# Attention denominators in a fused conv / linear attention / expert kernel: guard on ScalarE, power of minus one on GpSimd, in place of guard and reciprocal on VectorE

## Chip, cores, metric

One Trainium2 chip, one of its cores. The metric is the device time of one execution, in microseconds. An execution takes some 4.5 ms, and the executions shown of the kernel before lie within 0.07% of each other.

## What is computed

Sixteen images of 64 channels and 56x56 pixels pass three residual blocks: a convolution block, linear attention over the 3136 pixels (tokens) with 16 heads, and a block of 32 experts. The change touches the attention block only, and there the denominators:

```python
q = jax.nn.elu(q) + 1.0; k = jax.nn.elu(k) + 1.0
q_cos, q_sin = q * cos, q * sin; k_cos, k_sin = k * cos, k * sin
kv_cos = einsum('bshx,bshz->bhxz', k_cos, v); kv_sin = einsum('bshx,bshz->bhxz', k_sin, v)
qkv = einsum('bshx,bhxz->bshz', q_cos, kv_cos) + einsum('bshx,bhxz->bshz', q_sin, kv_sin)
denom = 1.0 / (einsum('bshd,bhd->bsh', q_cos, k_cos.sum(axis=1))
             + einsum('bshd,bhd->bsh', q_sin, k_sin.sum(axis=1)) + 1e-05)
o = qkv * denom[..., None]
out = o.reshape(b, s, h * d) @ dense_w.T + dense_b
```

The 1e-05 is "the guard", and 1/(...) the reciprocal.

## The kernel before

The images are worked on in eight **pairs**, two images on the 128 partitions. A hardware loop runs seven pairs ("loop"), the eighth is written out behind it ("last"). One pair has a k phase (key features and their products), a **q phase** and a tail (second layer norm, routing, then the convolution block of the next pair). The change lies in the q phase.

The q phase takes the pixels in chunks of 448 (8 rows of an image), 7 for each image, so 14 chunks, called s = 0 to 13 (`STEPS` is 14). The engines each run their own instruction queue in order, and a software pipeline over **steps** s = 0 to 16 is written out by hand in each of them. In step s, chunk s gets its query features, chunk s-1 its denominators, chunk s-2 is scaled and multiplied by the output matrices, and chunk s-3 is folded into the residual Y. Steps 14 to 16 drain the pipeline. Within a step a counter cc = 0 to 4 sets the places.

What happens to one chunk, by engine and line:

- TensorE projects the queries, in four parts of 256 features (L1375, banks A and B in turn, cc = 0 to 3). ScalarE takes exp (L688, into EQ), and VectorE makes the feature from both (L1010 `q_features`, into Q). L1010 empties the bank.
- TensorE forms partial denominators (L1392, bank E), VectorE multiplies them by cos and sin (L1027 `den_parts`, into DS), TensorE sums them (L1403 `q_sums`, into bank C, 96 partitions x 224 values: two halves of the chunk, 16 heads, in three copies).
- VectorE adds the guard (L1033 `den_guard`, bank C into RR[:, 0], which empties the bank) and takes the reciprocal (L1040 `den_reciprocal`, RR[:, 0] into RR[:, 1]).
- GpSimd splits the reciprocal in three bf16 parts, RS3 (L544, L546, L550, L551, L553: "the split").
- TensorE spreads the parts over the channels (L1417 `q_broadcast`, four times for a chunk, through bank C), and VectorE scales the features by it (L1019 `q_scale`, four times). "Broadcast cc" and "scale cc" below are the cc-th of these.
- TensorE multiplies the scaled features by the output matrices (L1428 `q_output`, bank D, once after each scale; "output cc"), VectorE multiplies by cos and sin (L1046 `out_parts`), TensorE folds (L1438 `q_fold`, bank C), and VectorE adds to Y (L1054 `out_residual`, "the residual").

Bank C is one PSUM area that serves these in a fixed order within a step: broadcast 0, sums, fold, broadcasts 1, 2, 3. Each use waits until the one before has been emptied. RR and RS3 are small SBUF tiles; RR has one buffer.

Between these, VectorE works through the depthwise convolution of the next pair (L855, in the seven loop pairs, 1, 1, 1, 2, 2 pieces at cc = 0 to 4; the last pair has none). In steps 12 and 14 these are replaced by parts of the second layer norm (L896 to L904), whose input comes through bank C at the end of steps 11 and 13 (TensorE L1264, ScalarE L589). In step 13 ScalarE takes the square root for it (L596 `deviations`, right after the exp of cc = 0), and VectorE applies it at cc = 2 (L916, L917). The square root and the exp need different function tables on ScalarE, so a table load stands ahead of each.

VectorE waits in L1010 at cc = 0, s >= 3, until output 3 of chunk s-3 is done, since both use the same buffer of Q.

## Time and profile before

| | |
|---|---|
| time, median of 3 | 4513.36 us (4513.25 to 4516.37) |
| profiled execution, its own time | 4506.9 us |
| its span | 4505.0 us |
| mean granted TensorE clock | 0.971 |
| PE / DVE / ACT / POOL busy | 3877.1 / 3434.0 / 1340.9 / 497.9 us |
| one steady step of the q phase (s = 3 to 11) | 18.2 us |

PE is TensorE's matmul pipe, PEld its weight load, DVE VectorE, ACT ScalarE, POOL GpSimd. "Busy" adds up over all stages, and stages have different limits. So the table says which engine works most over the whole, not which one sets the pace of the q phase. That is read in the rows below: from how long a step takes, and from the chain of work in it.

### The profile page before, as it was taken

Reading aid. Unit: us, or ns where it says so; the run is one execution under the profiler, and the core shown is the slowest. Engines: PE = TensorE matmul, PEld = TensorE weight load, DVE = VectorE, ACT = ScalarE, POOL = GpSimd, SP = SyncE. Lnnn points to the kernel's source line nnn. Section 1 sums busy time; section 2 is a strip of 40 time slices with the busy share of each in tenths; the row PEclk is TensorE's granted clock in tenths of the full one; section 3 lists DMA queues with packets and bytes.
Section 4 is the critical chain, followed back from the end, with each engine's and each line's share of the span. In section 5 each row is a group of like instructions: output and inputs, shape, how many; then the busy total and the mean of one; then the engine's idle time right before and its main releaser. Section 6 shows DMA issues by size and latency. Waiting matters only on the chain.

```text
span 4505.0 us, 48667 instructions
## 1 busy us (share of the span) xinstructions
PE 3877.1 (86%) x15836; PEld 1865.8 (41%) x15836; DVE 3434.0 (76%) x4533; ACT 1340.9 (30%) x1432; POOL 497.9 (11%) x977
## 2 busy tenths in 40 slices
PE   4998889987998889988899879988899888998876
PEld 2443344433543335433444335433354334443353
DVE  6688886888778886888868887788868888556633
ACT  0152233422253223522334222532235223342220
POOL 0011100111011110111001110111101110011100
PEclk8999999999999999999999999999999999999967
DMA  1000000000000001000000000000010000100035
GB/s 43 15 1 1 1 15 23 1 1 1 22 16 1 1 1 37 1 1 1 15 23 1 1 1 22 16 1 1 1 37 1 1 1 15 27 1 1 1 101 185
DMA packets 18779, 70.61 MB, mean 16 GB/s; under 512 B 8797, under 2 KB 13565, under 8 KB 13629
## 3 DMA queue, kind: packets, MB, share of 16 engines
q1 hardware_dynamic: 18509, 67.16, 4.8%
q8 instruction: 151, 2.47, 0.2%
q14 instruction: 119, 0.97, 0.1%
HBM read 37.32 MB, written 29.84 MB: 15 GB/s over the span
## 4 chain that ended last, share of the span: by engine, by line
PE 68%; DVE 19%; issue 8%; ACT 4%; DMA 1%; SPq 1%; DVEq 0%; ACTq 0%
PE ps_D L1428 16%; DVE region L1019 7%; PE ps_C L1346 6%; PE ps_D L1227 4%; PE ps_D L1346 4%; PE ps_E L1346 4%; PE ps_A L1331 4%; DVE arena L855 3%; PE ps_B L1331 3%; PE ps_A L1375 3%; PE ps_C L1253 3%; PE ps_C L1417 2%; PE ps_C L1403 2%; PE ps_C L1438 2%; PE ps_E L1392 2%
## 5 line engine op out<-in xcount | busy, mean ns | idle before, releaser
L1428 PE MATMUL ps_D<-region,small 128*128 128x448 f32 x1792 | 793.7, 567 | 171.5 <-DVE region L1019 171.5
L855 DVE SCALAR_TENSOR_TENSOR arena<-arena,W8C 128x448 f32<-128x448 f32 x1344 | 876.3, 692 | 0.9
L1428 PEld LDWEIGHTS ps_D<-region,small 128*128 128x128 f32 x1792 | 320.8, 193 | 535.1 <-DVE region L1019 349.2
L1019 DVE TENSOR_TENSOR region<-region,ps_C 128x896 f32<-128x896 f32 x400 | 433.1, 1083 | 80.8 <-PE ps_C L1417 69.3
L688 ACT ACTIVATE EQ<-ps_A,NEG 128x896 f32<-128x896 f32 x224 | 225.7, 1008 | 832.4 <-PE ps_A L1375 832.4
L532 POOL TENSOR_TENSOR UA<-region,CS 128x128 f32<-128x128 f32 (+1 forms) x400 | 192.0, 482 | 1924.6 <-DVE region L924 908.5
L688 ACT ACTIVATE EQ<-ps_B,NEG 128x896 f32<-128x896 f32 x224 | 225.6, 1007 | 598.1 <-PE ps_B L1375 598.0
L1346 PE MATMUL ps_C<-region,UA 128*128 128x512 f32 (+1 forms) x800 | 378.1, 595 | 0.0
L987 DVE SCALAR_TENSOR_TENSOR region<-region,ps_A 128x1024 f32<-128x1024 f32 (+1 forms) x200 | 243.8, 1219 | 122.8 <-ACT region L666 121.1
L987 DVE SCALAR_TENSOR_TENSOR region<-region,ps_B 128x1024 f32<-128x1024 f32 (+1 forms) x200 | 243.8, 1219 | 109.8 <-ACT region L666 107.4
L1010 DVE SCALAR_TENSOR_TENSOR region<-EQ,ps_A 128x896 f32<-128x896 f32 x224 | 242.6, 1083 | 82.5 <-ACT EQ L688 43.3
L666 ACT ACTIVATE region<-ps_A,NEG 128x1024 f32<-128x1024 f32 (+1 forms) x200 | 222.9, 1114 | 263.5 <-PE ps_A L1331 263.4
L666 ACT ACTIVATE region<-ps_B,NEG 128x1024 f32<-128x1024 f32 (+1 forms) x200 | 223.0, 1115 | 248.8 <-PE ps_B L1331 248.6
L544 POOL CAST RS<-RR 96x224 bf16<-96x224 f32 x112 | 57.1, 510 | 1829.0 <-DVE RR L1040 1813.3
L1403 PE MATMUL ps_C<-DS,SEL 128*96 128x224 f32 x448 | 118.2, 389 | 161.1 <-DVE region L1019 152.9
L1417 PE MATMUL ps_C<-RS,SELB 96*128 96x224 bf16 x1600 | 224.1, 263 | 29.4 <-ACT un L589 16.3
L1010 DVE SCALAR_TENSOR_TENSOR region<-EQ,ps_B 128x896 f32<-128x896 f32 x224 | 242.3, 1082 | 8.2 <-ACT EQ L688 7.1
L1392 PE MATMUL ps_E<-region,small 128*32 128x448 f32 x1792 | 214.9, 551 | 37.1 <-DVE region L1010 37.1
L1227 PE MATMUL ps_D<-region 112*128 112x512 f32 x496 | 214.8, 593 | 11.7 <-ACT region L631 11.7
L1417 PEld LDWEIGHTS ps_C<-RS,SELB 96*128 96x128 bf16 x1600 | 148.5, 99 | 180.2 <-issue 110.5
L1346 PE MATMUL ps_D<-region,UA 128*128 128x512 f32 (+1 forms) x400 | 205.9, 596 | 0.0
L1346 PE MATMUL ps_E<-region,UA 128*128 128x512 f32 (+1 forms) x400 | 204.2, 592 | 0.0
(310 smaller groups left out, 5792.4 us busy)
## 6 DMA issues: line engine op xcount, KB each, us to landing
arena<-x SPq DMA_DIRECT2D x8, 1568.0 KB, 6.8
t_keep<-Y SPq DMA_DIRECT2D x7, 1568.0 KB, 5.2
w_keep<-region SPq DMA_DIRECT2D x7, 784.0 KB, 5.9
CST<-t_keep SPq DMA_DIRECT2D x2, 1568.0 KB, 10.2
small<-t_keep SPq DMA_DIRECT2D x2, 1568.0 KB, 13.7
plane<-w_keep SPq DMA_DIRECT2D x4, 784.0 KB, 16.0
UHL<-t_keep SPq DMA_DIRECT2D x2, 1568.0 KB, 13.2
out<-CST SPq DMA_DIRECT2D x2, 1568.0 KB, 12.2
```

Source lines behind the costliest of these rows:

```text
L666: act.activation(E[0:r, k % 2], here.area(("kp", k))[0:r, :], ACT.Exp, bias=NEG1[0:r, 0:1]).then_inc(e_ready.sem, 1)
L688: act.activation(EQ[:, cc % 2], here.area(key)[:, :] .rearrange("p (c n) -> p c n", c=2)[:, :, 0:PIX], ACT.Exp, bias=NEG1[:, 0:1]).then_in ...
L855: dve.scalar_tensor_tensor(out=chunk, in0=window, scalar=w[:, k:k + 1], in1=chunk, op0=ALU.mult, op1=ALU.add).then_inc(taps_done.sem, 1)
L987: dve.scalar_tensor_tensor(out=KT[0:r, k % 3], in0=E[0:r, k % 2], scalar=1.0, in1=here.area(key)[0:r, :], op0=ALU.min, op1=ALU.max)\
L1010: dve.scalar_tensor_tensor(out=Q[s % 3][:, 2 * cc:2 * cc + 2, :], in0=EQ[:, cc % 2], scalar=1.0, in1=here.area(key)[:, :].rearrange("p (c ...
L1019: dve.tensor_tensor(out=q, in0=q, op=ALU.mult, in1=here.area(key)[:, :].rearrange("p (c n) -> p c n", c=2)[:, :, 0:PIX])\
L1227: ins = pe.matmul(here.area("t3")[:, :], UCOL[0:HALFP, j, :], UCOL[0:HALFP, j:j + 7:2, :], start=j == 0, stop=j == SPLIT - 1)
L1331: ins = pe.matmul(here.area(key)[0:r, cut], UTS[i][:, t * P:t * P + r], w[:, cut], start=m == 0, stop=m == 1)
L1346: ins = pe.matmul(dst, UA[0:r, k % 3].rearrange("p s c -> p (s c)"), KT[0:r, k % 3, n * 512:(n + 1) * 512], start=t == 0, stop=t == TILES - 1)
L1392: ins = pe.matmul(here.area(key)[j * STRIP:(j + 1) * STRIP, 0:PIX], KK[i][:, c, :], Q[s % 3][:, c, :], start=g == 0, stop=g == 1)
L1417: ins = pe.matmul(here.area(key)[:, at:at + SUB], SELB[:, j, 2 * c:2 * c + 2, :].rearrange("p h c -> p (h c)"), RS3[:, s % 2], start=True, ...
L1428: ins = pe.matmul(here.area(key)[:, 0:PIX], MW[i][:, c, :], Q[s % 3][:, c, :], start=c == 0, stop=c == NCHUNK - 1)
```

## The change

ScalarE adds the guard. It does so behind its exp of cc = 0, as an `Identity` activation with the 1e-05 as bias, from bank C into RR[:, 0], and that now empties the bank. It first waits for the split of the chunk before, since RR[:, 0] has one buffer. GpSimd then takes RR[:, 0] to the power of -1 (two-input instruction, the second input a broadcast column of -1) into RR[:, 1], ahead of its split. VectorE's two instructions are gone. Nothing else moves.

```diff
                 for s in range(STEPS):
+                    pool.wait_ge(*here.emptied(("dsum", s)))
+                    pool.tensor_tensor(out=RR[:, 1], in0=RR[:, 0], in1=NEG1[0:96, 0:1].broadcast_to([96, SUB]), op=ALU.pow).then_inc(recip_ready.sem, 1)
                     pool.wait_ge(*recip_ready.at(pair, s + 1))
...
+            def den_guard(here, s):
+                key = ("dsum", s)
+                if s >= 1:
+                    act.wait_ge(*split_ready.at(here.pair, s))
+                    passed(act)
+                act.wait_ge(*here.filled(key))
+                act.activation(RR[:, 0], here.area(key)[0:96, 0:SUB], ACT.Identity, bias=EPS[0:96, 0:1])\
+                    .then_inc(*here.empty(key))
...
                                            ACT.Exp, bias=NEG1[:, 0:1]).then_inc(eq_ready.sem, 1)
+                        if cc == 0 and 1 <= s <= STEPS:
+                            den_guard(here, s - 1)
                         if cc == 0 and s - 2 in LN2_STEPS[:2]:
                             deviations(ln2_sums, ln2_std, pair, LN2_STEPS.index(s - 2))
...
-            def den_guard(here, s):
-                dve.wait_ge(*here.filled(("dsum", s)))
-                dve.tensor_scalar(RR[:, 0], here.area(("dsum", s))[0:96, 0:SUB], DEN_EPS, None, ALU.add)\
-                    .then_inc(*here.empty(("dsum", s)))
-
-            def den_reciprocal(here, s):
-                dve.wait_ge(*here.emptied(("dsum", s)))
-                if s >= 1:
-                    dve.wait_ge(*split_ready.at(here.pair, s))
-                dve.reciprocal(RR[:, 1], RR[:, 0]).then_inc(recip_ready.sem, 1)
...
-                        if cc == 1 and 1 <= s <= STEPS:
-                            den_guard(here, s - 1)
                         if cc == 1 and s >= 3 and not drain:
                             out_residual(here, s - 3)
-                        if cc == (1 if drain else 2) and 1 <= s <= STEPS:
-                            den_reciprocal(here, s - 1)
```

The lines of the changed kernel are shifted: exp is L700 there, the guard L669, the square root L598, the power L540.

ScalarE's queue in step 13 of a loop pair, before (exp of cc = 0, square root with its table loads, exp of cc = 1 and 2):

```order
L688 ACTIVATE EQ<-ps_A,NEG1 128x896 [waits ps_A_filled]
L595 REGISTER_ALU
L596 ACT_TABLE_LOAD
L596 ACTIVATE ST<-ST,EPS 128x14 [waits ln2_sums]
L687 REGISTER_ALU
L688 ACT_TABLE_LOAD
L688 ACTIVATE EQ<-ps_B,NEG1 128x896 [waits ps_B_filled]
```

And in the changed kernel, same place:

```order
L700 ACTIVATE EQ<-ps_A,NEG1 128x896 [waits ps_A_filled]
L666 REGISTER_ALU
L668 REGISTER_ALU [waits split_ready]
L669 ACTIVATE RR<-ps_C,EPS 96x224 [waits ps_C_filled]
L597 REGISTER_ALU
L598 ACT_TABLE_LOAD
L598 ACTIVATE ST<-ST,EPS 128x14 [waits ln2_sums]
L699 REGISTER_ALU
L700 ACT_TABLE_LOAD
L700 ACTIVATE EQ<-ps_B,NEG1 128x896 [waits ps_B_filled]
```

The guard has come in between the exp of cc = 0 and all that follows it, the table loads, the square root and the exp of cc = 1, and it waits for the sums (ps_C_filled). In the other steps it stands at the same place, ahead of the exp of cc = 1, without table loads. No table load has been added anywhere in ScalarE's queue.

VectorE's queue in a steady step before, from the features of cc = 1 to those of cc = 2 and the reciprocal:

```order
L1010 SCALAR_TENSOR_TENSOR region<-EQ,ps_B 128x896 [waits eq_ready]
L1032 REGISTER_ALU
L1033 TENSOR_SCALAR RR<-ps_C 96x224 [waits ps_C_filled]
L1053 REGISTER_ALU
L1054 SCALAR_TENSOR_TENSOR Y<-ps_C,DBC,Y 64x448 [waits ps_C_filled]
L844 REGISTER_ALU
L855 SCALAR_TENSOR_TENSOR arena<-arena,W8C 128x448 [waits taps_done]
L1018 REGISTER_ALU
L1019 TENSOR_TENSOR region<-region,ps_C 128x896 [waits ps_C_filled]
L1007 REGISTER_ALU
L1010 SCALAR_TENSOR_TENSOR region<-EQ,ps_A 128x896 [waits eq_ready]
L1039 REGISTER_ALU [waits ps_C_emptied]
L1040 RECIPROCAL RR<-RR 96x224 [waits split_ready]
```

In the changed kernel the rows of L1032, L1033, L1039 and L1040 are missing there and the rest stands as it was; the residual (L1054) follows the features of cc = 1 directly. GpSimd's queue has the power ahead of each split:

```order
L539 REGISTER_ALU
L540 TENSOR_TENSOR RR<-RR,NEG1 96x224 [waits ps_C_emptied]
L541 REGISTER_ALU
L546 CAST RS3<-RR 96x224 [waits recip_ready]
L547 REGISTER_ALU
L548 TENSOR_TENSOR RR<-RR,RS3 96x224 [waits gstep]
```

Before, the first two of these rows were not there, and the cast waited for VectorE.

## Rows read from the trace of the kernel before

**Rows 1.** Profile page, busy time and share of the span by engine.
```profile
PE 3877.1 (86%) x15836; PEld 1865.8 (41%) x15836; DVE 3434.0 (76%) x4533; ACT 1340.9 (30%) x1432; POOL 497.9 (11%) x977
```

**Rows 2.** One step by windows: a loop pair's, the last pair's; busy us, PEclk.
```profile
core 0: us, PE busy (x) PEld busy (x) DVE busy (x) ACT busy (x) POOL busy (x), PEclk, DMA share, GB/s
432.39:450.61 18.22, 15.18 (x71) 6.82 (x70) 16.12 (x21) 4.03 (x4) 2.43 (x5) 1.00 0.00 1
4142.50:4160.92 18.42, 15.22 (x71) 6.83 (x72) 12.02 (x13) 4.03 (x5) 2.31 (x5) 1.00 0.00 1
```

**Rows 3.** Chain of work through that steady step: start us, us, what.
```profile
436.07 1.00 PE ps_C L1403 x4
...
440.83 1.10 DVE region L1019
...
444.93 1.10 DVE region L1019
...
449.87 1.72 PE ps_D L1428 x4
```

**Rows 4.** Timeline of the same step: start us, us, engine, line, operation, [idle before].
```profile
436.52 1.08 DVE L1010 SCALAR_TENSOR_TENSOR region<-EQ,ps_B 128x896 f32<-128x896 f32 x1
437.52 0.38 DVE L1033 TENSOR_SCALAR RR<-ps_C 96x224 f32<-96x224 f32 x1
...
439.50 0.68 DVE L1054 SCALAR_TENSOR_TENSOR Y<-ps_C,DBC,Y 64x448 f32<-64x448 f32 x1 [1.60 <-PE ps_C L1438]
...
444.62 0.49 POOL L544 CAST RS<-RR 96x224 bf16<-96x224 f32 x1 [15.41 <-DVE RR L1040]
...
446.82 0.60 POOL L553 TENSOR_TENSOR RS<-RR,RS 32x224 bf16<-32x224 f32 x1
```

**Rows 5.** Instructions by line: ns min/median/max, first and last start, form.
```profile
L1040 DVE RECIPROCAL RR<-RR x112: 1539/1542/1550, 372.5 to 4287.4; 96x224 f32<-96x224 f32 x112
L546 POOL TENSOR_TENSOR RR<-RR,RS x112: 605/607/1433, 374.9 to 4289.6; 96x224 f32<-96x224 f32 x112
...
L688 ACT ACTIVATE EQ<-ps_B,NEG x224: 1000/1007/1009, 358.3 to 4272.5; 128x896 f32<-128x896 f32 x112
...
L709 ACT ACTIVATE region<-ps_B,GBC x23: 629/630/632, 652.2 to 4328.9; 64x448 f32<-64x448 f32 x23
```

**Rows 6.** Timeline of step 12 of the first pair, and its clock by windows.
```profile
566.48 1.00 PE L1403 MATMUL ps_C<-DS,SEL 128*96 128x224 f32 x4 [2.33 <-DVE region L1019]
...
570.20 0.69 DVE L1054 SCALAR_TENSOR_TENSOR Y<-ps_C,DBC,Y 64x448 f32<-64x448 f32 x1 [1.06 <-PE ps_C L1438]
...
572.14 1.09 DVE L1019 TENSOR_TENSOR region<-region,ps_C 128x896 f32<-128x896 f32 x1
...
577.12 1.09 DVE L1019 TENSOR_TENSOR region<-region,ps_C 128x896 f32<-128x896 f32 x1 [0.49 <-DVE SQ L902]
...
578.26 3.23 PE L1428 MATMUL ps_D<-region,small 128*128 128x448 f32 x4 [2.07 <-DVE region L1019]
...
580.00:582.00 2.00, 2.00 (x7) 0.89 (x7) 0.20 (x1) 0.00 (x0) 0.00 (x0) 0.54 0.00 0
```

**Rows 7.** Timeline of step 13 of the first pair.
```profile
583.93 1.28 ACT L596 ACT_TABLE_LOAD   x1
...
586.85 1.01 ACT L688 ACTIVATE EQ<-ps_B,NEG 128x896 f32<-128x896 f32 x1
...
591.60 0.69 DVE L1054 SCALAR_TENSOR_TENSOR Y<-ps_C,DBC,Y 64x448 f32<-64x448 f32 x1 [1.60 <-PE ps_C L1438]
...
593.04 1.09 DVE L1019 TENSOR_TENSOR region<-region,ps_C 128x896 f32<-128x896 f32 x1
...
598.28 1.08 DVE L1019 TENSOR_TENSOR region<-region,ps_C 128x896 f32<-128x896 f32 x1
```

**Rows 8.** Timeline of steps 1 and 2 of the first pair.
```profile
368.25 0.99 PE L1403 MATMUL ps_C<-DS,SEL 128*96 128x224 f32 x4 [1.17 <-DVE DS L1027]
...
378.31 0.93 PE L1417 MATMUL ps_C<-RS,SELB 96*128 96x224 bf16 x4 [1.74 <-POOL RS L553]
...
380.11 1.07 DVE L1019 TENSOR_TENSOR region<-region,ps_C 128x896 f32<-128x896 f32 x1
```

## Prediction

> **What bounds the kernel now.** I read the busy times first. TensorE leads over the whole kernel, VectorE is second with 76% [rows 1], and inside the q phase VectorE is the fuller engine: 16.12 of 18.22 us of a steady step against TensorE's 15.18 [rows 2]. That makes relieving VectorE look worth while. The second row of the same view speaks against it. The last pair has no depthwise pieces, VectorE is busy for only 12.02 us there, and the step still takes 18.42 us. So four microseconds less VectorE work bought nothing. The steady step isn't limited by VectorE's amount of work.
>
> The chain of work shows what limits it [rows 3]. It goes sums, output 0, fold, broadcast 1, scale 1 (starts 440.83), output 1, projection, broadcast 2, scale 2 (444.93), output 2, broadcast 3, projection, partial denominators, output 3 (449.87 to 451.59), and through the features of cc = 0, the cos/sin product and scale 0 to the next sums. TensorE's instructions in order with VectorE's scales between them. In this step neither L1033 nor L1040 is in the chain. I call the start of the sums T; here T = 436.07 [rows 3], and the step repeats every 18.2 us.
>
> **Removing the reciprocal.** 112 reciprocals of 1.54 us [rows 5] and 112 guards of 0.38 us [rows 4] are 215 us of VectorE work. In a steady step the reciprocal stands between scale 1 and scale 2. Their distance is 4.10 us [rows 3], and TensorE fills it (output 1, projection, broadcast 2), so without the reciprocal VectorE would only wait there. Gain: 0.
>
> **Moving the guard.** What ended the guard's wait is no longer in VectorE's queue but in ScalarE's, ahead of the exp of cc = 1, which used to be ready early. What is queued behind it: that exp, then the features of cc = 1, then the residual on VectorE, and broadcast 1 on TensorE, which needs bank C back from the residual. Step by step from T: the sums take 1.00 us [rows 3]; 0.04 us to wake ScalarE (my allowance for a hand-over; the table says the same order for all of them); the guard; the exp, 1.01 us [rows 5]; 0.03 us; and the features, after which VectorE starts its next instruction 1.00 us later (436.52 to 437.52, [rows 4]). The guard's size isn't in the trace. An Identity with bias from PSUM takes 0.63 us for 448 columns and an exp 1.01 us for 896 [rows 5], 0.84 ns a column, which makes 0.44 us for 224. The two rows bound it, at 0.44 us by that line and 0.63 us by the larger Identity. I take 0.44. The sum is 1.00 + 0.04 + 0.44 + 1.01 + 0.03 + 1.00 = T + 3.52. The residual starts now at 439.50 = T + 3.43 [rows 4], held there by the fold, not by VectorE (1.60 us idle). So the new path is 0.09 us later, and if neighbouring ScalarE instructions overlap a little, equal. I take 0.05 us for each of the 72 steady steps (s = 3 to 11 of eight pairs): **+3.6 us**, bounds -7 (-0.1 a step; VectorE runs into fewer collisions) and +22 (+0.3 a step, the larger guard and slow hand-overs).
>
> **Step 12** is the one kind of step that VectorE does bound. The norm's parts stand in its queue, and scale 1 to scale 2 takes 572.14 to 577.12 = 4.98 us [rows 6] instead of 4.10 [rows 3]. Without the reciprocal TensorE's 4.10 becomes the distance: -0.88. The residual comes 3.72 us after the sums (566.48, 570.20) and could come at 3.52: -0.2. Together -1.1 in seven pairs, less in the last, about **-8 us**. Behind it hangs more. After the idle 2.07 us TensorE's granted clock is 0.54 in this stretch, near the lower level, 1.2 GHz, and output 2 takes 3.23 us [rows 6] where the same line has 1.72 us in a steady step [rows 3]. With the shorter gap this dip may go, some 1.6 us in each of 7 pairs: another **-11**. I think that likely (3 in 4).
>
> **Step 13** is where the new order hurts. ScalarE's square root stands behind the exp of cc = 0, with table loads on both sides. From the first load (583.93) to the exp of cc = 1 (586.85) pass 2.92 us [rows 7], and today they lie beside VectorE's and TensorE's work of the step's start. In the changed kernel they stand behind the guard, and that waits for the sums. So: 1.00 + 0.04 + 0.44 + 2.92 + 1.01 + 0.03 + 1.00 = T + 6.44 for the residual, which is at 591.60 today, T + 3.43 as ever: +3.0 us. The reciprocal's absence gives back part: scale 1 to scale 2 takes 5.24 us here (593.04 to 598.28, [rows 7]), and TensorE allows 4.10: -1.1. Net +1.9 in eight pairs: **+15 us**. TensorE idles for 3 us ahead of broadcast 1, longer than the 2.07 us after which it ran at 0.54 in step 12 [rows 6]. A dip of the same price, 1.6 us in eight pairs, is likely: **+13**. Bounds of the step: +12 and +30.
>
> **The power on GpSimd** has no row at all. The nearest is the two-input subtraction of the same shape on the same engine, 0.605 us [rows 5], and that is the lower end. [...] If that is ten such passes it takes 6 us, and at twenty 12 us. VectorE pays four times its simple instruction for the reciprocal (1.54 against 0.38), which would give 2.5 us here. I take 6 us and keep 0.6 to 12. When is it felt? In a steady step the power can start at about T + 1.7. The split after it takes 444.62 to 447.42 = 2.80 us [rows 4], with some 0.2 us of hand-overs. The next step's broadcast 0 comes behind output 3, at 451.5 = T + 15.4. So up to 10.7 us are free, and I cost it at nothing there; beyond that each microsecond lengthens every step by as much. In steps 1 and 2 there is less room: sums from 368.25, so the power starts at about 369.9, the split after it takes 3 to 4 us, and scale 0 at 380.11 needs broadcast 0 (0.93 us) to have begun by 379.1 [rows 8]. That leaves 5.1 to 6.2 us. With 6 us it costs 0.5 us a pair, a little more in the last: **+5**; at 3 us 0, at 10 us +36.
>
> The Trainium skill speaks against the move (GPSIMD Engine Reference, sections 3.1 and 4.1): elementwise work belongs on VectorE, GpSimd being about two times slower with two inputs, and a body with data-dependent branches costs about 12 cycles an element. Worked out from that page's 1.2 GHz, 224 elements would take 2.2 us, an estimate. By it the +5 above would be 0 and the time 4 or 5 us lower; no row here shows what the power's body is.
>
> **The sum.** 3.6 - 8 - 11 + 15 + 13 + 5 = +18 us. Leaving both clock terms out gives +16, so they hardly matter together, only if one comes without the other. Against the profiled execution's own 4506.9 us (span 4505.0) that is 4525; against the median, 6.5 us higher, 4531. I give 4530.
>
> **Rivals.**
> (a) *The relief counts: faster.* VectorE's queue would bind in the steady steps too, as it nearly does in loop pairs (16.12 of 18.22 busy). If all 1.92 us counted in the loop's 63 steady steps, it would be 4513 - 121 = 4392. It decides from the point where the residual after the guard is not held by the fold. The last pair's step of 18.42 us at 12.02 us busy [rows 2] speaks against it. A mild form is the step 12 term alone with its clock and a step 13 that costs little: -19 + 12 - 7 = -14, 4500. Together 0.12.
> (b) *No change.* The power is short (under 5 us), step 12 gives its 19 us back, and step 13 costs 15 without a dip: 3.6 - 19 + 15 = 0, so 4513. For it speaks that step 13 was idle for 2 us in places today without a dip. 0.26.
> (c) *GpSimd becomes the bound: much slower.* The power takes over 10.7 us. At 14 us each of some 100 steps is 3.3 us longer, +330, 4840. No row excludes it; only a body of more than seventeen elementary passes would do it. 0.14.
> (d) *The change doesn't do what it says*, by table loads around the new Identity. ScalarE's order shows none added, so under 0.01.
> (e) My forecast, with the power between 3 and 10.7 us and step 13 with or without a dip: 4522 to 4575. 0.48.
>
> **How the numbers follow.** Likeliest 4530. Range: down to the mild form of (a) and up to a power of nearly 10.7 us with the guard's upper bound: 4500 to 4590. That leaves out (c) and the strong form of (a). A difference under 0.2% (9 us) can't be told from none by a measurement of this kernel. Faster by more: 0.12. Within: 0.26. Slower: 0.62.
>
> **What would show it.** Right: the steady step stays at 18.2 to 18.3 us, with VectorE's busy time 1.9 us lower and an idle stretch of about 2 us ahead of the features of cc = 1, ended by the exp; step 12 shorter, by 1 us or by 2.7 with the full clock; step 13 longer by 2 to 4 us, with the table loads after the sums. Wrong: a steady step below 18 us would mean that VectorE had bound it; a steady step of 20 us or more with broadcast 0 waiting for L555 would mean a power over 10.7 us; and a residual later than T + 3.6 in the steady step would put the guard's path higher than I have it.

## The result: 62% slower, by the length of one GpSimd instruction

The changed kernel takes 7323.7 us (median of 4, 7321.6 to 7328.0) against 4513.3 us, a ratio of 1.623 with an interval of 1.620 to 1.626. That is 2810 us more. The forecast was 4530 us; the run went the way of rival (c), and much further than it was priced.

The page of the changed kernel: busy time and share of the span by engine; the granted clock in 40 slices; the chain by engine and line; and the costliest group (busy us, mean ns of one, idle before it).

```profile
PE 4100.0 (56%) x15836; PEld 1973.2 (27%) x15836; DVE 3237.5 (44%) x4309; ACT 1376.3 (19%) x1544; POOL 4494.1 (61%) x1089
...
PEclk9967789677986679866797668967789777987776
...
POOL 60%; issue 32%; PE 5%; DVE 1%; DMA 1%; POOLq 0%; ACT 0%; SPq 0%; DVEq 0%; ACTq 0%
...
L540 POOL TENSOR_TENSOR RR<-RR,NEG 96x224 f32<-96x224 f32 x112 | 4034.0, 36018 | 665.2 <-ACT RR L669 665.2
```

One power takes 36.0 us. GpSimd is the busiest engine with 61%, where it had 11% [rows 1], and the power alone is 4034 us in 112 instructions. VectorE has 224 instructions fewer, and its busy time fell by 197 us (3434.0 to 3237.5), somewhat less than the 215 us that the prediction had counted for them. Nobody profited.

One steady step of the changed kernel, timeline (start us, us, engine, line, operation, [idle before <- what ended it]):

```profile
585.46 0.44 ACT L669 ACTIVATE RR<-ps_C,EPS 96x224 f32<-96x224 f32 x1 [30.29 <-PE ps_C L1402]
585.98 36.02 POOL L540 TENSOR_TENSOR RR<-RR,NEG 96x224 f32<-96x224 f32 x1 [4.53 <-ACT RR L669]
...
589.30 0.56 PE L1416 MATMUL ps_C<-RS,SELB 96*128 96x224 bf16 x4
...
622.53 0.37 POOL L546 CAST RS<-RR 96x224 bf16<-96x224 f32 x1 [0.53 <-POOL RR L540]
...
624.60 0.60 POOL L555 TENSOR_TENSOR RS<-RR,RS 32x224 bf16<-32x224 f32 x1
625.25 0.93 PE L1416 MATMUL ps_C<-RS,SELB 96*128 96x224 bf16 x4 [24.62 <-POOL RS L555]
...
626.22 1.09 DVE L1033 TENSOR_TENSOR region<-region,ps_C 128x896 f32<-128x896 f32 x1 [23.93 <-PE ps_C L1416]
...
627.47 1.70 PE L1402 MATMUL ps_C<-DS,SEL 128*96 128x224 f32 x4
...
629.21 0.44 ACT L669 ACTIVATE RR<-ps_C,EPS 96x224 f32<-96x224 f32 x1 [30.12 <-PE ps_C L1402]
...
629.73 36.02 POOL L540 TENSOR_TENSOR RR<-RR,NEG 96x224 f32<-96x224 f32 x1 [4.53 <-ACT RR L669]
```

This is a closed loop: the power (36.02), the split (622.53 to 625.20), broadcast 0, scale 0, the sums, the guard, and the next power, 43.75 us after the last here, 43.46 in most steps and on average over the steady ones. All of TensorE's and VectorE's other work of a step has long been done when broadcast 0 waits 24.6 us for the split. After this pause TensorE runs slowly. Broadcast 0 takes 0.93 us where broadcast 1 of the step before took 0.56 (at 589.30), and the sums take 1.70 us instead of 1.00 [rows 3]. The windows show the granted clock: 0.50, the level of 1.2 GHz, from 625.2 to 629.2 us, and 1.00 from 588.4 to 600.0. The mean granted clock of the run is 0.787 against 0.971. The ScalarE wait of 30 us ahead of the guard costs nothing by itself; it is the same pause, seen from another queue.

The prediction had worked out that a step has room for a power of 10.7 us and that each microsecond beyond counts in full. 18.2 + (36.0 - 10.7) = 43.5 us, and 43.46 was measured. Times 111 that is 2808 us. So the mechanism was right, the threshold nearly so (experiment 3 puts it a little higher), and one number, the length of the power, was wrong by a factor of six.

That the sum meets the measurement to 0.04 us is in part luck. Its 10.7 came from three pieces of the loop outside the power: 1.7 us from the start of the sums to the power, 3.0 from the power to broadcast 0, and 2.8 from broadcast 0 to the next sums. In the step shown they are 2.26 (the sums before started at 583.72), 3.25 and 2.22 us, together 7.73 instead of 7.5, and 7.44 on average. The slow clock made the first longer, and the third is shorter since scale 0 no longer waits behind VectorE's other work.

### The profile page after: what moved, and what is told of

It is laid out like the page before. It is cut to its first block, busy times and chain, and to the rows that moved or that the text cites. A ratio compares the mean times of both kernels' runs of the same rounds, so it can differ in the third digit from the quotient of the medians.

```text
span 7326.2 us, 48856 instructions
## 1 busy us (share of the span) xinstructions
PE 4100.0 (56%) x15836; PEld 1973.2 (27%) x15836; DVE 3237.5 (44%) x4309; ACT 1376.3 (19%) x1544; POOL 4494.1 (61%) x1089
## 4 chain that ended last, share of the span: by engine, by line
POOL 60%; issue 32%; PE 5%; DVE 1%; DMA 1%; POOLq 0%; ACT 0%; SPq 0%; DVEq 0%; ACTq 0%
POOL RR L540 55%; POOL UA L532 2%; POOL RR L548 1%; POOL RS L555 1%; PE ps_C L1345 1%; POOL RS L553 1%; POOL RS L546 1%; PE ps_A L1530 0%; PE ps_D L1226 0%; PE ps_A L1330 0%; PE ps_D L1345 0%; PE ps_E L1345 0%; PE ps_B L1330 0%; PE ps_C L1402 0%; DMA plane<-w_keep 0%
## 5 line engine op out<-in xcount | busy, mean ns | idle before, releaser
L540 POOL TENSOR_TENSOR RR<-RR,NEG 96x224 f32<-96x224 f32 x112 | 4034.0, 36018 | 665.2 <-ACT RR L669 665.2
L1416 PE MATMUL ps_C<-RS,SELB 96*128 96x224 bf16 x1600 | 264.7, 297 | 2800.9 <-POOL RS L555 2777.9
L1033 DVE TENSOR_TENSOR region<-region,ps_C 128x896 f32<-128x896 f32 x400 | 435.0, 1088 | 2871.9 <-PE ps_C L1416 2863.1
L1427 PE MATMUL ps_D<-region,small 128*128 128x448 f32 x1792 | 842.5, 596 | 149.8 <-DVE region L1033 149.8
L869 DVE SCALAR_TENSOR_TENSOR arena<-arena,W8C 128x448 f32<-128x448 f32 x1344 | 858.6, 678 | 0.9
L669 ACT ACTIVATE RR<-ps_C,EPS 96x224 f32<-96x224 f32 x112 | 49.6, 443 | 3121.8 <-PE ps_C L1402 3121.8
L1427 PEld LDWEIGHTS ps_D<-region,small 128*128 128x128 f32 x1792 | 355.0, 212 | 547.8 <-DVE region L1033 330.2
L700 ACT ACTIVATE EQ<-ps_A,NEG 128x896 f32<-128x896 f32 x224 | 225.4, 1006 | 541.1 <-PE ps_A L1374 541.0
L700 ACT ACTIVATE EQ<-ps_B,NEG 128x896 f32<-128x896 f32 x224 | 224.1, 1000 | 366.8 <-PE ps_B L1374 366.7
## 6 DMA issues: line engine op xcount, KB each, us to landing
CST<-t_keep SPq DMA_DIRECT2D x2, 1568.0 KB, 10.7
```

Of the source, the lines that this page charges most:

```text
L540: pool.tensor_tensor(out=RR[:, 1], in0=RR[:, 0], in1=NEG1[0:96, 0:1].broadcast_to([96, SUB]), op=ALU.pow).then_inc(recip_ready.sem, 1)
L700: act.activation(EQ[:, cc % 2], here.area(key)[:, :] .rearrange("p (c n) -> p c n", c=2)[:, :, 0:PIX], ACT.Exp, bias=NEG1[:, 0:1]).then_in ...
L869: dve.scalar_tensor_tensor(out=chunk, in0=window, scalar=w[:, k:k + 1], in1=chunk, op0=ALU.mult, op1=ALU.add).then_inc(taps_done.sem, 1)
L1033: dve.tensor_tensor(out=q, in0=q, op=ALU.mult, in1=here.area(key)[:, :].rearrange("p (c n) -> p c n", c=2)[:, :, 0:PIX])\
L1416: ins = pe.matmul(here.area(key)[:, at:at + SUB], SELB[:, j, 2 * c:2 * c + 2, :].rearrange("p h c -> p (h c)"), RS3[:, s % 2], start=True, ...
L1427: ins = pe.matmul(here.area(key)[:, 0:PIX], MW[i][:, c, :], Q[s % 3][:, c, :], start=c == 0, stop=c == NCHUNK - 1)
```

## Experiments

**1. The power replaced by a multiplication.** Is the power the whole loss, and does the rest of the sum hold?

```diff
-pool.tensor_tensor(out=RR[:, 1], in0=RR[:, 0], in1=NEG1[0:96, 0:1].broadcast_to([96, SUB]), op=ALU.pow)
+pool.tensor_tensor(out=RR[:, 1], in0=RR[:, 0], in1=NEG1[0:96, 0:1].broadcast_to([96, SUB]), op=ALU.mult)
```

> The changed kernel, but GpSimd multiplies by -1 where it took the power of -1, so the reciprocal is left out and the denominators are wrong. Everything else of the change stays. Theory (the power's length is the whole loss, the rest of my sum holds): the multiplication takes 0.6 us, a steady step 18.2 to 18.3 us, step 12 is 1 to 2.7 us shorter and step 13 is 2 to 4 us longer than before; time 4513 + 3.6 - 8 - 11 + 15 + 13 = 4526, between 4505 and 4545. Rival (VectorE had bound the steady step after all, and only the power hid that): a steady step near 16.3 us and a time near 4392. Rival (the guard's new place costs by itself much more than I had it): over 4600.

Measured: 4557.9 us (5 runs), ratio 1.0096 (1.008 to 1.011), 41 us more than before on the same chip, and 13 us above the range expected. So some 98.5% of the loss is the power's length. It is the operation, too: the multiplication has the same operands, the broadcast column among them, and takes 0.56 us. The steady step is 18.21 us, as before and as forecast. Its timeline (same columns) and its windows row (span, then PE, PEld, DVE, ACT and POOL busy, PEclk):

```profile
437.74 1.00 PE L1402 MATMUL ps_C<-DS,SEL 128*96 128x224 f32 x4 [1.56 <-DVE region L1033]
438.78 0.44 ACT L669 ACTIVATE RR<-ps_C,EPS 96x224 f32<-96x224 f32 x1 [5.29 <-PE ps_C L1402]
439.12 0.99 ACT L700 ACTIVATE EQ<-ps_B,NEG 128x896 f32<-128x896 f32 x1
439.30 0.56 POOL L540 TENSOR_TENSOR RR<-RR,NEG 96x224 f32<-96x224 f32 x1 [14.13 <-ACT RR L669]
...
440.15 1.09 DVE L1024 SCALAR_TENSOR_TENSOR region<-EQ,ps_B 128x896 f32<-128x896 f32 x1 [1.87 <-ACT EQ L700]
...
441.18 0.68 DVE L1057 SCALAR_TENSOR_TENSOR Y<-ps_C,DBC,Y 64x448 f32<-64x448 f32 x1
```
```profile
434.50:452.71 18.21, 15.18 (x72) 6.82 (x71) 14.28 (x19) 4.36 (x5) 3.46 (x6) 1.00 0.00 1
```

The guard takes 0.44 us. The residual starts at 441.18, 3.44 us after the sums, where the kernel before had 3.43 [rows 3, 4]. VectorE's busy time in the step fell from 16.12 to 14.28 us; there is now a wait of 1.87 us ahead of the features of cc = 1, and the step is the same to a hundredth. The rival that VectorE had bound the steady step is out.

Step by step, from the distances between VectorE's cos/sin products of the denominators (L1027 before, L1041 here) in the second pair:

| stretch of one loop pair | before | multiplication |
|---|---|---|
| steps 1 and 2 | 11.08 + 17.25 | 10.57 + 16.29 |
| a steady step | 18.21 | 18.21 |
| step 12 | 24.22 | 21.62 |
| step 13 | 19.46 | 23.88 |
| step 14 to the next pair's step 1 | 289.8 | 295.8 |

Step 12 gains 2.6 us, the forecast with its clock term (2.7): output 2 behind a pause of 1.18 us takes 1.77 us there, at a granted clock of 1.00. Step 13 loses 4.4 us, of which 1.9 plus 1.6 were forecast. Its rows, from the first pair:

```profile
588.76 1.00 PE L1402 MATMUL ps_C<-DS,SEL 128*96 128x224 f32 x4 [1.56 <-DVE region L1033]
...
589.80 0.44 ACT L669 ACTIVATE RR<-ps_C,EPS 96x224 f32<-96x224 f32 x1 [5.29 <-PE ps_C L1402]
590.26 1.28 ACT L598 ACT_TABLE_LOAD   x1
...
591.88 1.28 ACT L700 ACT_TABLE_LOAD   x1
593.17 1.01 ACT L700 ACTIVATE EQ<-ps_B,NEG 128x896 f32<-128x896 f32 x1
...
595.33 0.69 DVE L1057 SCALAR_TENSOR_TENSOR Y<-ps_C,DBC,Y 64x448 f32<-64x448 f32 x1
...
596.08 0.93 PE L1416 MATMUL ps_C<-RS,SELB 96*128 96x224 bf16 x4 [3.06 <-DVE Y L1057]
```

Both table loads stand behind the guard, and the residual comes at T + 6.57 (worked out: 6.44). Broadcast 1 behind the 3.06 us pause takes 0.93 us, so the dip that was called likely was there.

The last line of the table was not in the prediction at all: 6 us in each of seven pairs, 43 of the 55 us that lie between the two profiled executions (spans 4505.0 and 4559.7 us). I come back to it in experiment 7.

**2. Half of the columns.** Does the power's length go by the columns, or is there a large fixed part? The power is on columns 0 to 111, the multiplication on the rest.

```diff
+pool.tensor_tensor(out=RR[:, 1, 0:112], in0=RR[:, 0, 0:112], in1=NEG1[0:96, 0:1].broadcast_to([96, 112]), op=ALU.pow)
+pool.tensor_tensor(out=RR[:, 1, 112:SUB], in0=RR[:, 0, 112:SUB], in1=NEG1[0:96, 0:1].broadcast_to([96, SUB - 112]), op=ALU.mult)
```

> The changed kernel with the power on the first 112 of 224 columns and a multiplication by -1 on the other 112; half of the reciprocals are left out. The kernel with a multiplication on all columns took 4558. Theory (160.8 ns for each column, no large fixed part; 10.7 us free in a step): the power takes 18.0 us, the multiplication some 0.35 us, and a steady step is 18.2 + (18.4 - 10.7) = 25.9 us; the time is 4558 plus 111 times 7.7 = 5410. Rival (a large fixed cost for each power, a program fetched for it, for instance): the power stays far above 18 us and the time lies nearer to 7324.

Measured: 5358.6 us, ratio 1.189 (1.187 to 1.191). The steady steps are 24.9 to 26.7 us long, 26.0 on average, where 25.9 was expected.

**3. 64 columns.** The same with 64 in place of 112 puts the power where the prediction had the threshold.

> The same with the power on 64 columns and a multiplication on 160; the other reciprocals are left out. Theory (10.7 us are free in a steady step, about 5.6 us in steps 1 and 2): power 10.3 us and multiplication 0.45 us, together 10.75, so a steady step of 18.2 to 18.4 us, step 1 to 2 longer by 5 us in each pair, time 4558 + 41 + up to 10 = 4599 to 4610. Rival (the power's length counts in full from the first microsecond, since GpSimd's queue is in series with the rest): 4558 plus 111 times 10.1 = 5680.

Measured: 4593.7 us, ratio 1.0194 (1.0181 to 1.0207). Against the multiplication's 1.0096 that is about 1% or 44 us more for 10.4 us more on GpSimd in each of 112 steps; in series it would have been over 1100. From step 5 on the steady steps are 18.21 us again. The cost sits in step 2, some 22.3 us in place of 16.3 in six of the eight pairs, and there in step 3 (18.9 to 20.4). The 44 us are a net figure: in the profiled executions steps 1 to 13 lost some 58 us against experiment 1, while the tail took 289.9 us in five of its six full intervals and gave 34 us back. Power and multiplication take 10.52 + 0.45 = 10.97 us. With 10.7 us free the steady step should have been 18.5 us. Broadcast 0 does wait 0.45 us for the split there, but scale 0 is still held by VectorE's other work:

```profile
475.13 0.56 PE L1417 MATMUL ps_C<-RS,SELB 96*128 96x224 bf16 x4 [0.45 <-POOL RS L556]
...
476.25 1.08 DVE L1034 TENSOR_TENSOR region<-region,ps_C 128x896 f32<-128x896 f32 x1
```

So about eleven microseconds are free in a steady step, a little more than the prediction had, and about five in the first ones, as it had it.

**4. A third of the partitions.** The power is on partitions 0 to 31, all columns; two multiplications do the other 64.

```diff
+pool.tensor_tensor(out=RR[0:32, 1], in0=RR[0:32, 0], in1=NEG1[0:32, 0:1].broadcast_to([32, SUB]), op=ALU.pow)
+pool.tensor_tensor(out=RR[32:64, 1], in0=RR[32:64, 0], in1=NEG1[32:64, 0:1].broadcast_to([32, SUB]), op=ALU.mult)
+pool.tensor_tensor(out=RR[64:96, 1], in0=RR[64:96, 0], in1=NEG1[64:96, 0:1].broadcast_to([32, SUB]), op=ALU.mult)
```

> The power on 32 of the 96 partitions, all 224 columns, and a multiplication by -1 on the other 64 in two instructions of 32 partitions (the reciprocals there are left out). Theory (the length goes by columns only): the power takes 36.0 us as in the changed kernel, the time is 7324 plus 112 times 1.2 us of multiplications = 7460. Rival (the length goes by the number of values): 12 us, a step of 18.2 + (13.2 - 10.7) = 20.7 us, time near 4840.

Measured: 7507 us (one run), 47 us above the 7460 expected. The power keeps its length. The power in the changed kernel and in experiments 2 to 4 (line, ns min/median/max, first and last start, form):

```profile
L540 POOL TENSOR_TENSOR RR<-RR,NEG x112: 36017/36017/36027, 369.1 to 7076.2; 96x224 f32<-96x224 f32 x112
```
```profile
L540 POOL TENSOR_TENSOR RR<-RR,NEG x112: 18197/18197/18207, 370.8 to 5125.1; 96x112 f32<-96x112 f32 x112
```
```profile
L540 POOL TENSOR_TENSOR RR<-RR,NEG x112: 10524/10525/10535, 369.5 to 4365.7; 96x64 f32<-96x64 f32 x112
```
```profile
L540 POOL TENSOR_TENSOR RR<-RR,NEG x112: 36005/36006/36015, 369.4 to 7252.5; 32x224 f32<-32x224 f32 x112
```

(36.017 - 18.197) / 112 = 159 ns a column, (18.197 - 10.525) / 48 = 160 ns, and 0.3 us are left as a fixed part. A third of the partitions takes the same time.

**5. The guard on ScalarE alone.** The reciprocal stays on VectorE, so only the guard's new place is measured.

```diff
 # ScalarE, behind the exp of cc = 0
+den_guard(here, s - 1)
 # VectorE
-den_guard(here, s - 1)
```

> Only the guard moves to ScalarE, at the place that it has in the changed kernel; the reciprocal stays on VectorE at the place of before, and GpSimd does the split alone. Theory (my working of the guard's path): steady step 18.2 to 18.3 us (+3.6 us in all), step 13 longer by 3.0 us and perhaps by another 1.6 us by the clock, since the reciprocal's absence gives nothing back; time 4513 + 4 + 24 = 4541, up to 4554. Rival (ScalarE has so much room, 30% busy, that moving the guard is free): 4513 plus or minus 5.

Measured: 4563.2 us, ratio 1.0107 (1.0089 to 1.0124), 47 us more than before, where 28 to 41 were expected. Steady steps 18.21 us: the guard's path is free there. The two profiled executions lie 55 us apart. Step 13 takes 22.8 to 24.2 us in the loop pairs against 19.46, so 3.3 to 4.7 us more, and 22.1 against 19.9 in the last, 29 us in all. Steps 1 and 2 are together 10 us longer over the eight pairs, for which the prediction had nothing. The tail adds 17 us: it was 295.8 us in three of the seven intervals, 289.3 in three, and 286.8 in the last one (before: 287.1), which has the written-out pair behind it. The guard's path through a steady step was sized well; the guard is a loss mostly by its place in step 13.

**6. The guard one place later,** behind the exp of cc = 1, with the multiplication in place of the power.

```diff
-if cc == 0 and 1 <= s <= STEPS:
+if cc == 1 and 1 <= s <= STEPS:
     den_guard(here, s - 1)
```

> The changed kernel with the multiplication by -1 in place of the power (reciprocal left out), and the guard one place later in ScalarE's queue, behind the exp of cc = 1. Theory (step 13 is longer because table loads, square root and exp stand behind the guard's wait): step 13 falls from 23.9 us to 18.4 or below, since those no longer wait for the sums and VectorE's reciprocal is gone; steps 12 and the steady ones keep their 21.6 and 18.2 us. Rival (step 13 is long for another reason, the shorter step 12 or the clock): it stays above 22 us.

Measured: 4477.8 us, ratio 0.991 (0.989 to 0.993), faster than before by 0.9%, without the reciprocal. Step 13 is 18.33 us in every loop pair. Step 12, which I had expected to stay at 21.6 us, takes 23.2 in most pairs. Of the 79 us between the profiled executions of this kernel and of experiment 1, 45 are step 13 and 39 are the tail, which ran at 289.4 us in all intervals but the first. ScalarE's rows in step 13:

```profile
582.52 1.28 ACT L598 ACT_TABLE_LOAD   x1
...
584.14 1.28 ACT L700 ACT_TABLE_LOAD   x1
...
585.43 1.01 ACT L700 ACTIVATE EQ<-ps_B,NEG 128x896 f32<-128x896 f32 x1
...
587.79 0.44 ACT L669 ACTIVATE RR<-ps_C,EPS 96x224 f32<-96x224 f32 x1 [1.35 <-PE ps_C L1402]
```

Loads and exp are done before the sums are, and the guard waits for them with nothing urgent behind it. The cause of the longer step 13 is thereby shown: the place in the queue, not the table loads as such.

**7. The tail.** Its work is the same in all these kernels. Two windows of 24 us that begin some 4 us ahead of the token pooling, in the kernel before and with the multiplication (busy us by engine, PEclk):

```profile
1213.60:1237.60 24.00, 23.32 (x118) 14.88 (x117) 4.51 (x13) 1.61 (x3) 0.00 (x0) 1.00 0.00 1
```
```profile
1225.49:1249.49 24.00, 23.33 (x101) 16.99 (x100) 3.88 (x12) 1.61 (x3) 0.00 (x0) 0.72 0.00 1
```

And the 64-column matmuls of the token pooling that stand there, before and with the multiplication (ns min/median/max):

```profile
L1300 PE MATMUL ps_E<-region,un x350: 272/275/320, 692.2 to 3851.9; 128*128 128x64 f32 x168, 64*128 64x64 f32 x7
```
```profile
L1299 PE MATMUL ps_E<-region,un x350: 275/421/473, 697.0 to 3902.1; 128*128 128x64 f32 x168, 64*128 64x64 f32 x7
```

TensorE was busy 97% of both windows, at clocks of 1.00 and 0.72, and got 118 matmuls done in one and 101 in the other. In all seven tails of the multiplication the clock fell within a microsecond of the first matmul of the pooling. Ahead of that matmul TensorE pauses twice, 0.45 and 0.22 us, with the clock at 1.00, and it has the same pauses in the kernel before, where the clock stays. The fall costs 6 us. I thought that fuller work in between would hold the clock up, and put six matmuls of 128x448 f16 into the pooling.

```diff
     ins = pe.matmul(here.area("pool")[:, 0:C], UT[2][0:r, t, :], WT[0:r, t, :], start=t == 0, stop=t == TILES - 1)
+    if t in (5, 11, 17) and here.span == "loop":
+        for a in range(2):
+            pe.matmul(ps["D"][:, 0:PIX], WQH[:, 0:P], WKH[:, 0:PIX], start=True, stop=True)
```

> The kernel with the multiplication (reciprocal left out), and in the tail of each loop pair six more matmuls of 128x448 f16 (two each at three places among the 25 64-column matmuls of the token pooling), whose result nobody reads. The kernel without them spends 295.8 us from the last cos/sin product of denominators of a pair to the first of the next, the kernel before 289.7 us, and the granted clock in the pooling and the first convolutions is 0.70 to 0.73 against 1.00. Theory (the clock falls there when the stretch of small matmuls meets it at a bad phase, and fuller work keeps it up): the stretch takes 289.7 + 6 x 0.19 = 290.8 us at clock 1.00, and the kernel's time falls by 7 times 5 = 35 us against the one without. Rival (the tail is longer for a reason of the change itself): it stays near 296 or becomes 297 us.

Measured: 4577.3 us, ratio 1.0125 (1.0102 to 1.0147), and the tail took 298.5 us in its six full intervals. The fillers added their own time and held nothing. But they came too late to test the theory. The first matmul of the pooling, the first two fillers, and the clock by windows (PEclk is the third number from the end):

```profile
1237.27 2.07 PE L1299 MATMUL ps_E<-region,un 128*128 128x64 f32 x12 [0.22 <-ACT region L625]
1239.12 0.95 PE L1303 MATMUL ps_D<-WKH,WQH 128*128 128x448 f16 x2
```
```profile
1235.10:1237.10 2.00, 1.49 (x19) 1.09 (x17) 1.32 (x6) 1.57 (x3) 0.00 (x0) 1.00 0.04 8
1237.10:1239.10 2.00, 1.83 (x12) 1.84 (x13) 0.85 (x3) 0.04 (x1) 0.00 (x0) 0.75 0.00 0
1239.10:1241.10 2.00, 2.00 (x11) 1.74 (x10) 0.00 (x0) 0.00 (x0) 0.00 (x0) 0.50 0.00 0
```

The clock had fallen before the first filler ran. So the experiment shows only that fillers behind the fall don't bring the clock back sooner; whether fuller work ahead of it would have held the clock stays untested. What stays is the observation: in the profiled execution of the kernel before all seven tails ran at full clock (289.7), with the multiplication none did (295.8), and with the guard alone four did and three didn't, within one execution and with the same instructions. What decides it isn't settled.

**8. Scale 0 first.** The chain of the kernel before [rows 3] has TensorE's longest idle stretch, 1.56 us, ahead of the sums, behind three VectorE instructions of which only the last, scale 0, is needed. If the step is this chain, reordering them should pay where taking away work doesn't. Guard and reciprocal are on VectorE, as before.

```diff
+q_scale(here, s - 2, 0)
-q_features(here, s, 0)
 out_parts(here, s - 3)
-q_scale(here, s - 2, 0)
+q_features(here, s, 0)
```

> The kernel before (guard and reciprocal on VectorE) with one thing reordered: at the start of a step (cc = 0, steps 2 to 13) VectorE does scale 0 first, then the cos/sin product of the outputs, then the features of cc = 0; before, the features came first and the scale last. Theory (the steady step is TensorE's chain with VectorE's scales in it, and its longest idle stretch, 1.56 us ahead of the sums, is VectorE's three instructions): scale 0 starts as soon as broadcast 0 is done, at 433.78 instead of 434.94, so a step is shorter by about 1.1 us and the time by 1.1 times 80 = 90 us, near 4425. Rival (VectorE's amount of work bounds the loop pairs' steps, 16.1 of 18.2 us): the step gets only some 0.3 us shorter there and 1.1 us in the last pair alone, time near 4480.

Measured: 4519.5 us, ratio 1.0029 (1.0018 to 1.004), slightly slower. The step went to 18.06 us in the loop pairs and 17.6 in the last one. The steps of the profiled execution gained 32 us in all, and its tails of 296 to 299 us took back 58. My expectation of 17.1 us was wrong. A row of the loop pair's step tells why:

```profile
436.85 0.97 PE L1440 MATMUL ps_C<-OS,FOLD 128*64 128x448 f32 x2 [0.92 <-DVE RR L1033]
```

The sums come a microsecond earlier, and now the fold waits 0.92 us for VectorE's guard to empty bank C, since the guard still stands behind the same queue. With the fillers of experiment 7 added it was 4528 us, ratio 1.000 (0.997 to 1.003). Eleven of its twelve executions lay between 4474 and 4536 us. In the profiled one a single tail ran at full clock, so this one says no more of the fillers than experiment 7 does. What was expected of it:

> The reordered kernel (guard and reciprocal on VectorE, scale 0 first), with the same six matmuls in the tail. Without them it was 0.3% slower than the kernel before, with steps shorter by 0.15 to 0.8 us and a tail of 296 to 299 us. Theory (it was slower only by the clock in the tail): tail 291 us, time 0.6 to 1.0% below the kernel before. Rival (the fillers don't hold the clock): slower than before by 0.3 to 0.5%.

**9. Scale 0 first, on the changed kernel with the multiplication.**

```diff
-if feature and cc < 4:
-    q_features(here, s, cc)
+if scaled and cc == 0 and not drain:
+    q_scale(here, s - 2, 0)
 if cc == 0 and s >= 3 and not drain:
     out_parts(here, s - 3)
-if scaled and cc == 0:
+if feature and cc < 4:
+    q_features(here, s, cc)
+if scaled and cc == 0 and drain:
     q_scale(here, s - 2, 0)
...
-pool.tensor_tensor(out=RR[:, 1], in0=RR[:, 0], in1=NEG1[0:96, 0:1].broadcast_to([96, SUB]), op=ALU.pow)
+pool.tensor_tensor(out=RR[:, 1], in0=RR[:, 0], in1=NEG1[0:96, 0:1].broadcast_to([96, SUB]), op=ALU.mult)
```

> The changed kernel with the multiplication by -1 in place of the power (reciprocal left out) and, in addition, scale 0 first in VectorE's step, as in the reordered kernel. That kernel's steady step was 18.06 us in loop pairs and 17.6 us in the last pair, where VectorE has no depthwise pieces. Theory (once TensorE's chain is shorter, VectorE's amount of work is the next bound, and only then its relief is worth something): with 1.9 us less on VectorE the loop pairs' step falls to 17.6 to 17.7 us, as in the last pair. Rival (something else holds the loop pairs' step): it stays at 18.06 us. The guard's path adds at most 0.1 us in either case.

Measured: 4437.9 us, ratio 0.982 (0.980 to 0.985). The step fell to 17.07 us, further than the theory said. That left two readings: less work on VectorE, or the guard no longer in its queue.

**10. A complete kernel from the parts.** The guard on ScalarE behind the exp of cc = 1, the reciprocal on VectorE, scale 0 first. It also separates the two readings, for here VectorE keeps 1.54 us of the 1.92.

Against the changed kernel, beside the reordering shown in experiment 9:

```diff
 # GpSimd
-pool.tensor_tensor(out=RR[:, 1], in0=RR[:, 0], in1=NEG1[0:96, 0:1].broadcast_to([96, SUB]), op=ALU.pow)
 # ScalarE
-if cc == 0 and 1 <= s <= STEPS:
+if cc == 1 and 1 <= s <= STEPS:
     den_guard(here, s - 1)
 # VectorE
+def den_reciprocal(here, s):
+    dve.wait_ge(*here.emptied(("dsum", s)))
+    if s >= 1:
+        dve.wait_ge(*split_ready.at(here.pair, s))
+    dve.reciprocal(RR[:, 1], RR[:, 0]).then_inc(recip_ready.sem, 1)
...
+if cc == (1 if drain else 2) and 1 <= s <= STEPS:
+    den_reciprocal(here, s - 1)
```

> A complete kernel made of what the runs so far showed: the guard on ScalarE, but behind the exp of cc = 1; the reciprocal on VectorE as before; scale 0 first in VectorE's step. Theory (the steady step is TensorE's chain; in the reordered kernel the fold waited 0.92 us for VectorE's guard, and with the guard on ScalarE that wait goes; the reciprocal lies beside TensorE's 4.1 us and costs nothing): steady step 17.1 to 17.3 us, step 13 not above 20 us, tail 290 to 299 us by the clock; time 1.0 to 1.8% below the kernel before. Rival (VectorE's amount of work, 15.7 us with the reciprocal, holds the step of the loop pairs): steady step 17.7 to 18.0 us, time 0 to 0.6% below.

Measured: 4393.9 us (4392.6 to 4396.9), ratio 0.973 (0.971 to 0.974), 2.7% faster than before, with the whole computation in it. That is more than the 1.0 to 1.8% expected: the tails kept the full clock (289.7 to 290.0 us, as before), and step 12 takes 20.5 us instead of 24.2. The gain isn't made by the tail's clock: the steps carry all of it. The steady step is 17.07 us with the reciprocal as it was without it. Its windows row (one step: span, then PE, PEld, DVE, ACT and POOL busy) and timeline:

```profile
432.52:449.59 17.07, 15.18 (x71) 6.81 (x71) 15.81 (x20) 4.47 (x6) 2.42 (x5) 1.00 0.00 1
```
```profile
432.52 1.00 PE L1410 MATMUL ps_C<-DS,SEL 128*96 128x224 f32 x4 [0.42 <-DVE region L1031]
...
433.55 0.44 ACT L667 ACTIVATE RR<-ps_C,EPS 96x224 f32<-96x224 f32 x1 [0.41 <-PE ps_C L1410]
...
434.95 0.97 PE L1445 MATMUL ps_C<-OS,FOLD 128*64 128x448 f32 x2
...
435.95 0.68 DVE L1061 SCALAR_TENSOR_TENSOR Y<-ps_C,DBC,Y 64x448 f32<-64x448 f32 x1 [0.37 <-PE ps_C L1445]
...
439.28 1.54 DVE L1047 RECIPROCAL RR<-RR 96x224 f32<-96x224 f32 x1
```

The fold follows output 0 without a wait, and TensorE's idle time ahead of the sums is 0.42 us in place of 1.56. The four combinations give the steady step of a loop pair: neither 18.21 us, guard on ScalarE alone 18.21, scale 0 first alone 18.06, both 17.07. Each edit alone is worth next to nothing since the other one's wait takes over. The reciprocal on VectorE costs the steady step nothing where it was tried both ways: 18.21 us with the guard on ScalarE alone, 17.07 with both.

**11. VectorE's guard with GpSimd's power.** The ScalarE part undone.

```diff
 # ScalarE, behind the exp of cc = 0
-den_guard(here, s - 1)
 # VectorE, behind the features of cc = 1
+def den_guard(here, s):
+    if s >= 1:
+        dve.wait_ge(*split_ready.at(here.pair, s))
+        passed(dve)
+    dve.wait_ge(*here.filled(("dsum", s)))
+    dve.tensor_scalar(RR[:, 0], here.area(("dsum", s))[0:96, 0:SUB], DEN_EPS, None, ALU.add)
...
+if cc == 1 and 1 <= s <= STEPS:
+    den_guard(here, s - 1)
```

> The change with its ScalarE part undone: VectorE adds the guard where it did before (now waiting for the split of the chunk before, since RR[:, 0] has one buffer), and GpSimd takes the power. Theory (the power alone closes the loop power, split, broadcast 0, scale 0, sums, guard): a step of 43.4 us and 7320 us, within 30 us of the changed kernel. Rival (the guard behind the exp on ScalarE has a share in the loss): lower by over 100 us.

Measured: 7418 us, ratio 1.642 (1.638 to 1.646), 95 us slower than the changed kernel, with steps mostly of 44.17 us. I had expected the same time. In a loop that GpSimd closes, everything between sums and power counts, and VectorE's guard stands behind the features of cc = 1: sums from 588.42, guard only at 590.71.

```profile
588.42 1.70 PE L1400 MATMUL ps_C<-DS,SEL 128*96 128x224 f32 x4
589.71 1.09 DVE L1012 SCALAR_TENSOR_TENSOR region<-EQ,ps_B 128x896 f32<-128x896 f32 x1 [0.85 <-ACT EQ L690]
590.71 0.38 DVE L1038 TENSOR_SCALAR RR<-ps_C 96x224 f32<-96x224 f32 x1
591.17 36.02 POOL L540 TENSOR_TENSOR RR<-RR,NEG 96x224 f32<-96x224 f32 x1 [5.02 <-DVE RR L1038]
```

The place on ScalarE is thus worth 0.7 us a step once the loop is the limit (44.13 against 43.46 on average).

## Why the prediction was wrong, point by point

- **The step that failed: the size of the power.** "If that is ten such passes it takes 6 us, and at twenty 12 us. [...] I take 6 us and keep 0.6 to 12." It takes 36.0 us, 160 ns a column, as much as sixty passes of the 0.605 us subtraction [rows 5]. No run shows ten passes or any other number of them, nor how the power is computed; the runs show only its length. VectorE's ratio of four between its reciprocal and a simple instruction didn't carry over either: on GpSimd the power takes 65 times the 0.56 us of the multiplication. The upper end was a guess at a number of passes, not a bound from a row, and I then used it as a bound: the range ended below it, at a power of nearly 10.7 us. The sentence "No row excludes it" stood right there under rival (c). With no row for the price and one whole engine in a closed loop, the honest chance for (c) was nearer to a half than 0.14, and its price open upward.
- **The estimate by the Trainium skill** (2.2 us, GPSIMD Engine Reference, section 3.1, branches at 12 cycles an element) was off by a factor of sixteen. The Trainium skill's advice against the move (GPSIMD Engine Reference, section 4.1) was right in direction, but its factor of two is given for add, multiply and maximum, and the measurement decides.
- **Slope: right. Threshold: nearly.** One for one beyond the room: 17.45 us more on GpSimd from experiment 2 to the changed kernel made the step 17.48 us longer (25.98 to 43.46). The room is somewhat larger than 10.7 us, since 10.97 us cost a steady step nothing in experiment 3; that 43.5 met 43.46 so closely is partly luck, by pieces that were off both ways. The first steps' smaller room (5.1 to 6.2 us) shows in the same experiment: 10.97 us made step 2 longer by 6.0.
- **VectorE's relief is worth nothing in the steady step: right.** 18.21 us with 1.8 us less work. The row of the last pair [rows 2] had said so.
- **The guard's path, T + 3.52 against 3.43: right,** measured 3.44, with a guard of 0.44 us as worked out from two other shapes. The steady step of 18.21 us didn't change; only the two steps ahead of step 12 grew, from 18.32 to 18.41 us, 1.4 us in all where I had 3.6.
- **Step 12: right** (-2.6 us in the second pair and -18 us over all eight, against -19, the clock term included). **Step 13: right in mechanism,** a little small: 4.4 us against 3.5 with the dip, 35 us against 28.
- **Steps 1 and 2**: with a short instruction they gain about 1.4 us in six pairs and lose 1.1 in the first and in the last, -6 us in all, where I had 0.
- **Missing from the sum: the tail's clock**, 6 us a pair in experiment 1. Over all pairs of the two profiled executions the steps add up to 1 - 18 + 35 - 6 = +12 us. The forecast without its power term had +13, but with errors that cancel, which is luck. With the tail's 43 us that makes 55, the difference of the two spans. I had priced the clock only where the change touches the work, and it answered in a place that the change doesn't touch.

## What to carry to other kernels

An operation for which the trace has no row needs a bound that comes from a measurement of that operation on that engine. Until there is one, its price is open upward, and what counts is how much room there is around it: that room can be worked out well beforehand (10.7 us here), and it should be compared with a one-off measurement before anything else is planned. In a loop of engines that wait for each other, look for which instruction of a queue is needed first, not for how busy the queue is: two moves, worth 0.0 and 0.15 us alone, gave 1.14 us of 18.21 together. And a small instruction moved into another engine's queue brings its wait along, so place it behind what is due earlier.

## What the runs showed of the hardware that I had not expected

- GpSimd's two-input power of f32: 159 to 160 ns a column plus 0.3 us, the same for 32 and for 96 partitions and the same to 0.01 us in all 112 instructions of a run, against 0.56 us for a multiplication of the whole 96x224 and 1.54 us for VectorE's reciprocal of it.
- TensorE's granted clock was 0.72 over 24 us in which TensorE was busy for 97%. It fell to 0.50 within a microsecond of the start of a stretch of 64-column matmuls, behind pauses of 0.45 and 0.22 us, in some passes through the same instructions and not in others. Six larger matmuls that ran behind the fall didn't bring it back sooner.
- A ScalarE Identity with bias from PSUM, 96x224, takes 0.44 us, on the line through 0.63 us for 448 columns and 1.01 us for an exp of 896.
